# A graph-network kernel on one core: registers of the edge loop loaded first, its ranks restarted sooner, one attention head's columns on VectorE

## The reference, cut to what matters

```python
# block 0: edge MLP, sum by source node, and matching of the two half graphs
m = relu(relu(concatenate([x[row], x[col]]) @ Wm1 + bm1) @ Wm2 + bm2)   # 16384 x 256
m_sum = segment_sum(m, row)
out = relu(relu(concatenate([x, m_sum, match(x)]) @ Wn1 + bn1) @ Wn2 + bn2)
# block 1: three attention layers (GAT), 4 heads of 32 columns, edges and loops
e = leaky_relu(al_s[src] + al_d[dst], 0.2)
alpha = exp(e - segment_max(e, dst)[dst]); alpha = alpha / segment_sum(alpha, dst)[dst]
h = segment_sum(h[src] * alpha, dst)      # layer norm and relu between layers
# block 2: mean over the first 10 neighbours of each source node (by rank), then @ W.T + b
keep = rank(edge within its row) < 10
# block 3: x + segment_sum(edge_weight * x[src], dst), then a two-layer MLP
```

## Time and profile before

| | before |
|---|---|
| median of 3 runs | 969.1 us (968.7 to 970.39) |
| profiled execution: time | 963.45 us |
| profiled execution: span | 961.5 us, 18681 instructions |
| PE busy | 881.2 us, 92% |
| DVE busy | 665.9 us, 69% |
| ACT busy | 502.8 us, 52% |
| POOL busy | 298.3 us, 31% |
| mean granted clock of PE | 0.984 |

### The profile page before, as it was taken

One profiled execution on the slowest core, in us unless ns is written; L12 is line 12 of the kernel. 1 busy time (PEld: TensorE's weight loads), 2 busy tenths in 40 slices (PEclk: granted clock), 3 DMA queues, 4 the chain that ended last, 5 costly groups with the idle time before them and its releaser, 6 DMA issues.

```text
span 961.5 us, 18681 instructions
## 1 busy us (share of the span) xinstructions
PE 881.2 (92%) x5491; PEld 547.6 (57%) x5526; DVE 665.9 (69%) x1778; ACT 502.8 (52%) x1009; POOL 298.3 (31%) x433
## 2 busy tenths in 40 slices
PE   8899959999899989998999988989998998899898
PEld 4657638878787878787878745422242222322244
DVE  6899966666666666666666764677767785967651
ACT  6421115555555656565555564666655665566621
POOL 8030075545454545454544400011132110112000
PEclk9999959999999999999999999999999999999999
DMA  3120041111211111111111300000000000000220
GB/s 83 47 66 1 0 154 55 44 66 44 66 44 66 44 66 44 66 44 66 44 60 44 70 2 1 1 1 1 1 1 0 1 1 0 1 1 0 86 90 22
DMA packets 19145, 35.87 MB, mean 37 GB/s; under 512 B 5280, under 2 KB 11552, under 8 KB 18976
## 3 DMA queue, kind: packets, MB, share of 16 engines
q0 software_dynamic: 7104, 19.41, 6.9%
q1 hardware_dynamic: 12000, 15.95, 4.9%
HBM read 29.56 MB, written 5.79 MB: 37 GB/s over the span
## 4 chain that ended last, share of the span: by engine, by line
PE 75%; DVE 13%; ACT 5%; issue 3%; DMA 1%; POOL 1%; DVEq 0%; ACTq 0%; POOLq 0%
PE PS L1420 9%; PE PS L1282 7%; PE PS L1276 6%; PE PS L1201 5%; PE PS L1405 5%; PE PS L1202 5%; PE PS L1149 5%; PE PS L1216 5%; PE PS L1411 4%; PE PS L1273 3%; PE PS L1323 3%; DVE OHd L998 3%; PE PS L1194 3%; PE PS L1374 2%; PE PS L1207 2%
## 5 line engine op out<-in xcount | busy, mean ns | idle before, releaser
L403 POOL DMA_INDIRECT BT<-Qtab,gidx x148 | 150.1, 1014 | 96.3 <-DVE gidx L825 61.1
L555 ACT ACTIVATE OHe<-OHs,sew 128x128 bf16<-128x128 bf16 x408 | 126.6, 389 | 62.1 <-PE PS L1282 61.6
L417 POOL TENSOR_SCALAR KV<-BT,pid 128x256 bf16<-128x256 uint8 x74 | 69.9, 945 | 175.0 <-DVE MS L900 169.5
L998 DVE CUSTOM_DVE_ANT_0 OHd<-PS,n1T 128x1024 bf16<-128x1024 f32 x96 | 112.1, 1220 | 9.5 <-PE PS L1374 9.5
L566 ACT ACTIVATE m2s<-m2s 128x512 f32<-128x512 f32 x68 | 42.8, 630 | 108.5 <-DVE m2s L926 108.5
L940 DVE TENSOR_SCALAR OHd<-iotaN,dstf 128x1024 bf16<-128x1024 f16 x136 | 63.9, 509 | 36.8 <-PE PS L1282 36.8
L926 DVE TENSOR_TENSOR m2s<-PS,bm 128x512 f32<-128x512 f32 x68 | 47.0, 691 | 54.1 <-PE PS L1202 54.1
L1201 PE MATMUL PS<-Wm,m1T 128*128 128x256 f32 x276 | 83.2, 384 | 0.0
L1202 PE MATMUL PS<-Wm,m1T 128*128 128x256 f32 x276 | 83.0, 383 | 0.0
L456 POOL TENSOR_TENSOR zl<-AL,Sx 128x8 f32<-128x8 f32 x12 | 2.6, 215 | 254.8 <-DVE Sx L998 254.8
L1282 PE MATMUL PS<-OHs,m2s 128*128 128x128 f32 x544 | 79.4, 290 | 0.0
(11 more groups left out here) (354 smaller groups left out, 1729.8 us busy)
## 6 DMA issues: line engine op xcount, KB each, us to landing
BT<-Wtab SPq DMA_DIRECT2D x1, 4096.0 KB, 12.8
BT<-Qtab,gidx POOLq DMA_INDIRECT x148, 2.8
BT<-Stab SPq DMA_DIRECT2D x1, 2048.0 KB, 10.4
Wtab<-H SPq DMA_DIRECT2D x4, 512.0 KB, 2.8
Wtab<-cs SPq DMA_DIRECT2D x4, 512.0 KB, 2.8
Qtab<-BT SPq DMA_DIRECT2D x1, 1024.0 KB, 4.5
Wn<-in_L_gnn_Wn SPq DMA_DIRECT2D x1, 1024.0 KB, 5.3
x<-in_x SPq DMA_DIRECT2D x1, 512.0 KB, 4.2
```

The lines of the kernel that those rows point to most:

```text
L403: g.indirect_dma_start(out=G[:, p % SLOTS, k, :], out_offset=None, in_=Qtab, in_offset=bass.IndirectOffsetOnAxis(ap=gidx[:, p, k:k + 1], a ...
L555: a.activation(OHe[:, k, j, :], OHs[:, k, :], ACT.Copy, scale=sew[:, j, bass.ds(2 * g + k, 1)])
L998: v.tensor_tensor_reduce(junk[n % 2], bank(4, 2), mask[:, i, :], 1.0, 2 * FAR, ALU.subtract, ALU.max, Sx[:, i, hd:hd + 1]).then_inc(S("gat ...
```

## The change

It has three parts.

1. *Edge loop, head of the body.* PE waits for `spans`, does the `value_load` and names slot, block and the two ends of the inner loop (`snap`) before it waits for `ranks_read` and issues the second three rank matmuls.
2. *Edge loop, end of a block.* PE waits for `msum_out` alone and restarts the ranks of the next block at once. The first of these matmuls starts its bank anew, so bank 4 is not cleared any more: four zero matmuls instead of five, and none after the last block. ACT copies `msum` before `TT`.
3. *Attention, head 0 of each layer.* DVE does the column operations before its last maximum of head 0, and then itself the 8 small operations that make `Apad` of this head; POOL does so for heads 1 to 3 only, and clears `Apad` once, much earlier. PE does the last head's distance row behind the bound row of head 0, halves swapped, and ACT copies it behind `rowA`; ACT does `ramp(0, 1)` ahead of `rowA`.

The diff, cut to its core (left out: the three lines on POOL that move the clearing of `Apad` and its wait):

```diff
                     g.sem_inc(S("lone_added"), 1)
-                for hd in range(HEADS):
+                for hd in range(1, HEADS):
                     n = HEADS * l + hd
                     i = n % 2
-                    if hd == 0:
+                    if hd == 1:
                         eng.wait_ge(S("gat_ext"), 3 * l + 3)
...
+                a.activation(msum[:, :, b * P:(b + 1) * P], bank(4)[:, 0:F2].rearrange("p (f n) -> p f n", f=2),
+                             ACT.Copy)\
+                    .then_inc(S("msum_out"), 1)
...
-                a.activation(msum[:, :, b * P:(b + 1) * P], bank(4)[:, 0:F2].rearrange("p (f n) -> p f n", f=2),
-                             ACT.Copy)\
-                    .then_inc(S("msum_out"), 1)
...
             for l in range(3):
-                def distance_out(hd):
-
-                    for half in range(2):
-                        eng.wait_ge(S("drow_done"), 2 * (HEADS * l + hd) + half + 1)
+                def distance_out(hd, halves=(0, 1)):
+
+                    for i, half in enumerate(halves):
+                        eng.wait_ge(S("drow_done"), 2 * (HEADS * l + hd) + i + 1)
                         a.activation(drow[hd][:, half * BANK:(half + 1) * BANK], bank(6 + half), ACT.Copy,
...
                     a.activation(AL[:, 3 * i:3 * i + nb, :], ext[:, :, D:EXT], ACT.Copy).then_inc(S("gat_ext"), 1)
-                for hd in range(1, HEADS):
+                for hd in range(1, HEADS - 1):
                     distance_out(hd)
...
                 eng.wait_ge(S("banks_clear"), l + 1)
+                ramp(0, 1)
                 for hd in range(HEADS):
...
                     a.activation(rowA[:, hd % 2, :], bank(6 + hd % 2), ACT.Copy).then_inc(S("rowA_out"), 1)
+                    if hd == 0:
+                        distance_out(HEADS - 1, (1, 0))
                     for j in range(NB):
                         n = HEADS * NB * l + NB * hd + j
-                        if j + 1 < NB:
+                        if j + 1 < NB and hd + j:
                             ramp(hd, j + 1)
...
-                for i in range(NB):
+                for i in range(NB - 1):
                     greatest(0, i)
...
                 eng.wait_ge(S("cols_ready"), l + 1)
+                greatest(0, NB - 1)
+                eng.wait_ge(S("gat_smax"), HEADS * NB * l + NB)
+                dcol = AL[:, :, HEADS]
+                link(v.tensor_tensor(zl[:, 0, :], dcol, Sx[:, :, 0], ALU.add))
+                link(v.scalar_tensor_tensor(lz[:, 0, :], zl[:, 0, :], SLOPE, zl[:, 0, :], ALU.mult, ALU.max))
+                link(v.tensor_tensor(Acol[:, 0, :], dcol, lz[:, 0, :], ALU.subtract))
+                if l:
+                    eng.wait_ge(S("rowT_done"), HEADS * l)
+                for k in range(3):
+                    last = v.tensor_copy(Apart(k), halved(Acol[:, 0, :]))
+                    if k < 2:
+                        link(last)
+                        link(v.tensor_tensor(halved(Acol[:, 0, :]), halved(Acol[:, 0, :]), Apart(k), ALU.subtract))
+                last.then_inc(S("row_parts"), 1)
                 between = {0: (0, 1), 1: (2, 3), 2: (4, 5), 3: (6,), 4: (7,)}
...
-            def ranks(pairs):
-
-                for region, tri, k in pairs:
+            def ranks(pairs, anew=False):
+
+                for i, (region, tri, k) in enumerate(pairs):
                     last = t.matmul(bank(4)[:, F2 + region * P:F2 + (region + 1) * P], tri[:], OHs[:, k, :],
-                                    start=False, stop=False, skip_group_check=True)
+                                    start=anew and i == 0, stop=False, skip_group_check=True)
                 return last
+
+            def restarted():
+
+                ranks(((0, beforeb, 0), (1, onesb, 0), (1, beforeb, 1)), anew=True).then_inc(S("ranks_restarted"), 1)
...
             g0, end = 0, last_pair(eng, 0)
-            for b in range(NB):
-                eng.wait_ge(S("src_onehots"), g0 + 1)
-                ranks(((0, beforeb, 0), (1, onesb, 0), (1, beforeb, 1))).then_inc(S("ranks_restarted"), 1)
+            eng.wait_ge(S("src_onehots"), 1)
+            restarted()
+            for b in range(NB):
                 with eng.Fori(g0, end) as g:
+                    eng.wait_ge(S("spans"), 1)
+                    span = eng.value_load(rngi[0:1, bass.ds(g, 1)], min_val=1, max_val=NB * NB * NB - 1)
+                    slot, first = eng.snap((g + 2) & (SLOTS - 1)), eng.snap((span >> 6) & (NB - 1))
+                    least, past = eng.snap((span >> 3) & 7), eng.snap((span & 7) + 1)
                     eng.wait_ge(S("ranks_read"), g + 1)
                     ranks(((0, notbefb, 0), (0, onesb, 1), (1, notbefb, 1))).then_inc(S("ranks_added"), 1)
-                    eng.wait_ge(S("spans"), 1)
-                    span = eng.value_load(rngi[0:1, bass.ds(g, 1)], min_val=1, max_val=NB * NB * NB - 1)
                     eng.wait_ge(S("turned_onehots"), g + 3)
-                    sources((g + 2) & (SLOTS - 1), (span >> 6) & (NB - 1))
+                    sources(slot, first)
...
                     eng.wait_ge(S("counts_ready"), g + 1)
-                    with eng.Fori((span >> 3) & 7, (span & 7) + 1, 2) as d:
+                    with eng.Fori(least, past, 2) as d:
                         for k in range(2):
...
                 after = last_pair(eng, b + 1) if b + 1 < NB else None
+                eng.wait_ge(S("msum_out"), b + 1)
+                if b + 1 < NB:
+                    restarted()
+                eng.wait_ge(S("weights_out"), b + 1)
                 eng.wait_ge(S("counts_out"), b + 1)
-                eng.wait_ge(S("msum_out"), b + 1)
-                for k in range(5):
-                    t.matmul(bank(k), zeros[:, 0:P], zeros[:, 0:BANK], start=True, stop=True)
+                if b + 1 < NB:
+                    for k in range(4):
+                        t.matmul(bank(k), zeros[:, 0:P], zeros[:, 0:BANK], start=True, stop=True)
                 g0, end = end, after
...
                     for half in range(2):
-                        if hd:
+                        if hd == HEADS - 1:
+                            half = 1 - half
+                            if half == 0:
+                                eng.wait_ge(S("rowA_out"), HEADS * l + 1)
+                        elif hd:
                             eng.wait_ge(S("drow_out"), 2 * (HEADS * l + hd) - 1 + half)
...
                     last.then_inc(S("rowT_done"), 1)
-                    eng.wait_ge(S("rowA_out"), HEADS * l + hd + 1)
...
                 source_row(1)
-                distance_row(3)
-                eng.wait_ge(S("drow_out"), 2 * (HEADS * l + HEADS))
+                eng.wait_ge(S("drow_out"), 2 * (HEADS * l + HEADS - 1))
                 for hd in range(HEADS):
                     bound_row(hd)
+                    if hd == 0:
+                        distance_row(HEADS - 1)
+                    eng.wait_ge(S("rowA_out"), HEADS * l + hd + 1)
                     for j in range(NB):
                         bounded(hd, j)
+                        if hd == 0 and j == 1:
+                            eng.wait_ge(S("drow_out"), 2 * (HEADS * l + HEADS))
                         if hd or j:
```

More of the change, by code:

```diff
@@ L374, in _ @@
             g.sem_inc(S("first_bias_parts"), 1)
+            g.memset(Apad[:], 0.0)
             eng.wait_ge(S("wg_loaded"), 16 * 17)
@@ L437, in _ @@
             link = Chain(eng, S("pool_chain"))
-            link(g.memset(Apad[:], 0.0))
             for l in range(3):
@@ L460, in _ @@
                     link(g.tensor_tensor(Acol[:, i, :], dcol, lz[:, i, :], ALU.subtract))
-                    if n:
-                        eng.wait_ge(S("rowT_done"), n)
+                    eng.wait_ge(S("rowT_done"), n)
                     for k in range(3):
```

## The result

The changed kernel takes 932.06 us (median of 4 runs, 928.02 to 933.86), the kernel before beside it 969.75. The ratio is 0.960, with a 95% interval of 0.955 to 0.964. Measured once more later, it was 0.959 (0.956 to 0.962). The forecast was 933.3.

The account below looks back on a forecast made before the run. The prediction took TensorE's edge loop, with gaps from late instruction issue behind the rank wait, as the bound. Gains of 24.4 + 3.6 + 5.7 + 2.1 = 35.8 us took 969.1 to 933.3 us, range 926 to 951.

Parts of the forecast that it names:

- The load behind the wait for the ranks: Edge loop: register load issued after the rank wait makes the gaps; moved ahead, 0.80 us goes from behind the wait.
- The body: Edge loop, ordinary body: falls from 5.47 to 5.0 us, 0.47 saved each.
- lower bound: Edge loop, ordinary body: 4.94 us if no gap is left in TensorE's work.
- upper bound: Edge loop, ordinary body: 5.14 us if the 0.46 from OHs to the closing step is time to issue.
- the loop over two bodies: Edge loop, TensorE's instruction issue: a chain through two bodies, put at 10.28 us.
- Ordinary, second and two-pass bodies: Edge loop, 52 bodies neither first nor last of a block: 0.47 us saved each, 24.4 us.
- block ends and first bodies: Edge loop: last bodies of a block save 8 x 0.45 = 3.6 us, first bodies 8 x 0.71 = 5.7 us.
- edit 3: Attention, first head of each of 3 layers: reordered work gains 0.7 us a layer, 2.1 us in all.
- Edit 2: Edge loop, block ends: earlier rank restart, one zero matmul less and swapped ACT copies are worth 0.
- B: Edge loop: another engine takes over as bound, via `m2_ready` or DVE's chain; body 5.25, 948 us; chance 0.10.
- C: Edge loop: only block starts gain, ordinary bodies stay at 5.47; 8 us saved with attention, 961 us; chance 0.12.
- D: Edge loop: the load ahead of the ranks starves PE, making the kernel slower, 990 us; chance 0.02.

Follow-up runs that it names:

- experiment 1: The kernel before with only the spans wait and register load moved ahead of the second rank matmuls: 933.89 us, ratio 0.960.
- (2): The changed kernel with the register load put back behind the second rank matmuls, the other two parts kept: 967.72 us, ratio 0.995.
- experiment 5: The changed kernel with the load of the span done twice at the body's head: 948.61 us, ratio 0.980.
- experiment 7: The changed kernel with the span loaded into a register without the bounds check behind the load: 926.90 us, ratio 0.958.
- experiment 6: The changed kernel with the four fields forced into registers at the body's head by a register move: 920.57 us, ratio 0.952.
- experiment 3: The changed kernel with the attention part of the diff undone, both edge loop parts kept: 933.87 us, ratio 0.960.
- experiment 10: The changed kernel with one of VectorE's maxima of head 1 moved behind head 0's third tile: 927.04 us, ratio 0.955.
- experiment 4: The kernel before, unchanged, measured and traced once more: 969.37 us, ratio 0.998.
- experiment 11: The changed kernel, measured and traced once more without any change: 932.41 us, ratio 0.959.
- experiment 9: The changed kernel with fields in registers at the body's head and no bounds check behind the load: 924.69 us, ratio 0.951.

## Why the prediction was right, and where it was not

**The load behind the wait for the ranks was the cause.** Moved alone it gives the whole ratio (experiment 1), put back it takes it away (2), doubled it costs again (5). The Trainium skill's sentence (Perfetto Trace Analysis, Tensor Engine Instruction), by which a waiting matmul doesn't hold up the sequencer, isn't borne out for these matmuls: in all 68 bodies of experiment 7 and in all of before the sequencer stood at them until DVE's read was over, and the reversal of edit 1 costs 3.6%. These waits compare with a register (`g + 1`); a wait for a constant wasn't tried.

**The body** came out at 5.06 where 5.0 was taken, within 4.94 to 5.14. The lower bound was 0.06 too low: the eight L1304 records take 0.95, not 0.89 (307.56 to the next rank matmul at 308.50). For the upper bound I took 0.46 from the end of OHs to the closing of the body as time to issue. In the changed kernel OHs ends at 302.81 + 0.41 = 303.22 and the closing step L1277 stands at 303.4:

```profile
L1277 PEldq ALU_OP  x2: 36/36/36, 303.4 to 308.6; - x2
```

That is some 0.2. With it the loop over two bodies is 10.28 - 0.26 = 10.02, just at what PE needs. This is the mis-sized term. It answers for experiment 5: 10.02 and the 0.65 of a second load are 10.67, and 10.74 was measured. Of experiment 6 it is one half of the answer. The other is that the fields cost less than was expected: by the medians of the two traces they take 0.78 us more ahead of the ranks and give back 0.47 between ranks and counts and 0.22 in the counts' own steps, so the loop grows by 0.09 and not by 0.3 to 0.4. That makes 10.11, a body of 5.06, where 5.03 was measured. Load and rank wait still end together, so this loop has no slack either: 22 of the 42 ordinary bodies stay above 5.00, and leaving out the check (7) ends that.

**The terms of the sum.** Ordinary, second and two-pass bodies gave 20.8 of 24.4; block ends and first bodies 7.7 of the 9.3 for both terms (one first head and one last body lie outside the steps counted). Second bodies save only 0.3 of 0.47: they start without a lead, and PE waits for `m2s` there (six times, 1.5 us in all), a wait that is gone without the check. Some 2.8 us of what the loop's terms lack come with edit 3 (experiment 3): the sum had nothing for what it does to the edge loop, and no run shows how it does it. Edit 2: 0, as said. Edit 3 in its own place: 0.93 to 0.99 a layer where 0.7 stood. The mechanism was right (bound row 2.05 sooner, half given back at DVE's third tile, shown by experiment 10); the 8 operations take 1.58, not 1.8, so DVE's tile comes no later than before instead of 0.3.

**What the sum left out** is the clock first of all. In the three traces with the load behind the ranks, 12 of 24 first bodies ran at the lower level; in the eight with the load first and the fields, or all but one, where they are used, 12 of 64; in the three with all fields in registers, 1 of 24. Three of these are of block 0, where the clock was low already before the loop: one in the changed kernel's first trace, one in experiment 7, and the 1 of 24. Each costs some 1.2 us: 4 of 8 against 1.5 of 8 is 3 us a run, an estimate. In attention, the first head of a layer ran at the lower level in 4 of 12 layers without edit 3 (92.6 instead of 90.9) and in none of 30 with it. This is one of the four, in layer 1 of experiment 4:

```profile
736.39 3.57 PE L1405 MATMUL PS<-BT,ident 128*128 128x512 f32 x4 [0.40 <-ACT PS L648]
```

The earlier trace rows have 1.98 for the same four. That is some 1.7 us a run. The counts go with a shorter gap (1.38 to 0.6 us between ranks and `sources`); that the gap is the cause wasn't tested by itself. The sum also left out the late steps behind bodies with two passes: 2.6 us in two of the three traces with the load behind the ranks and in none of the others, so some 1.7 a run. Between the edge loop and the first attention layer the clock fell only in kernels with the load first: from the last `sources` to the first maximum it is 68.2 to 68.3 us in those three traces and 70.2 to 70.9 in three of the eleven others (68.0 to 68.4 in the rest); between 515 and 585 us the granted clock is 0.93 in experiment 11 and 1.00 in the changed kernel's first trace. That is some 0.7 us a run.

So the 933.3 was hit by errors of opposite sign: 4.8 too much in the sum's terms, and by this estimate some 5.7 us (3 + 1.7 + 1.7 - 0.7) that it did not count. That the total came within 1.3 us is luck; what the runs bear out is the mechanism and the size of its main term.

**The rivals.** B (another engine) doesn't hold in the changed kernel beyond second bodies, but appeared for one block in experiment 9, through `m2_ready` as described. C and D are out: the load doesn't starve PE, even twice.

## What to carry to other kernels

An engine's sequencer is a resource with its own chain: where it stands at a wait for another engine, work that depends on nothing there (register loads, checks, address steps) belongs ahead of the wait, and the price is read from register records and starts of matmuls, not from busy time. Look at what was built: a named value may still be computed where it is used, and forcing it into a register was worth 0.8% more. And set two traces of the same kernel side by side before a difference of one per cent is put down to a term: here they differed by 6.8 us.

## What the hardware showed that I had not expected

VectorE's OHd build takes longer where it overlaps with GpSimd's L418. In the edge loop of the changed kernel 117 of 134 OHd records do so and take 601 ns in the mean, the other 17 take 503; before, 62 overlap with 547 ns and 72 don't with 474. The page of the profile has for OHd 589 ns in the mean (509 before) and for L418 1007 ns (945 before):

```profile
L942 DVE TENSOR_SCALAR OHd<-iotaN,dstf 128x1024 bf16<-128x1024 f16 x136 | 74.8, 589 | 9.9 <-PE PS L1304 9.9
...
L418 POOL TENSOR_SCALAR KV<-BT,pid 128x256 bf16<-128x256 uint8 x74 | 74.5, 1007 | 139.2 <-DVE MS L902 132.4
```

The Trainium skill (GPSIMD Engine Reference, Specifications, the row on SBUF interfaces) says that the two share their SBUF interfaces and contend when DVE is in a two-port mode or has two SBUF inputs. The trace agrees for DVE, with the 601 against 503 ns. For L418 it is not clear: before, it takes 945 ns with and without an overlap; in the changed kernel 1017 with and 947 without. In which mode DVE works here no run shows.

In the body shown, the two OHd take 1.15 us together, 0.94 in the earlier trace rows, and DVE's rank read ends 1.14 ahead of the ranks (304.70 to 305.84) where 1.3 was forecast. And a clock that has fallen to 0.57 behind a block's end is at 1.00 again in the next window, 4 us later: the loss is one body, not a block.
